# Windowed attention on one core: scores and transposes in smaller tiles, group norm folded into the evacuations, the subtraction of the maxima divided between two engines

## What is computed

```
x = x + L0(gn(x))      # windows of 7x7: layer norm, a linear scan over 49 steps, an MLP with gelu
x = x + L1(gn(x))      # shifted-window attention

# L1, for every 7x7 window (49 tokens) of the image rolled by 3:
qkv  = xw @ qkv_w.T + qkv_b            # 12 heads of 16 channels
attn = (q * 16**-0.5) @ k.T + bias + mask
out  = softmax(attn) @ v
out  = out @ proj_w.T + proj_b         # rolled back
```

## The kernel before, in words

| p | order on TensorE before |
|---|---|
| 0 | scores, transposes, mix 0, turn 0, value group, turn 1 |
| 1 | scores, transposes, project 0, project 1, value group |
| 2 | scores, transposes, project 2, values 0, value group |
| 3 | scores, transposes, values 1, value group, wait for keys and queries, mix 1 |

## Time and profile before

### The profile page before, as it was taken

One profiled execution on the slowest core, in us unless ns is written; L12 is line 12 of the kernel. 1 busy time (PEld: TensorE's weight loads), 2 busy tenths in 40 slices (PEclk: granted clock), 3 DMA queues, 4 the chain that ended last, 5 costly groups with the idle time before them and its releaser, 6 DMA issues. The chain is left out here.

```text
span 4769.8 us, 122473 instructions
## 1 busy us (share of the span) xinstructions
PE 4471.3 (94%) x42440; PEld 3822.0 (80%) x42440; DVE 4085.7 (86%) x7841; ACT 2351.8 (49%) x4594; POOL 2642.9 (55%) x1714
## 2 busy tenths in 40 slices
PE   0599999999999999999969999999999999999998
PEld 0488888888888888888857888888888888888887
DVE  6798888888888888888838888888888888888887
ACT  0244444444444444444415555555555555555555
POOL 1245555455545554555536666666666666666665
PEclk9999999999999999999969999999999999999999
DMA  8011111111111111111112222222222222222222
GB/s 341 21 38 38 39 39 41 37 39 39 41 37 39 39 41 38 38 39 39 37 46 79 80 78 79 81 81 77 80 79 81 77 81 78 82 80 78 79 81 65
DMA packets 398996, 310.66 MB, mean 65 GB/s; under 512 B 140011, under 2 KB 397243, under 8 KB 397755
## 3 DMA queue, kind: packets, MB, share of 16 engines
q1 hardware_dynamic: 396212, 307.89, 21.9%
q10 hardware_dynamic: 2736, 2.14, 0.1%
HBM read 145.48 MB, written 87.33 MB: 49 GB/s over the span
## 5 line engine op out<-in xcount | busy, mean ns | idle before, releaser
L885 POOL TENSOR_TENSOR E<-E,ri 128x588 f32<-128x588 f32 x512 | 802.8, 1568 | 781.5 <-DVE ri L1092 781.5
L604 PE MATMUL ps_o<-w,g_hi 128*128 128x384 f32 x2352 | 709.7, 365 | 5.9 <-DVE g_lo L544 4.1
L416 ACT ACTIVATE gF<-ps_g,b1f 128x512 f32<-128x512 f32 x588 | 404.6, 688 | 392.8 <-PE ps_g L635 390.7
L604 PE MATMUL ps_o<-w,g_lo 128*128 128x192 f32 x2352 | 534.5, 254 | 0.0
L969 ACT ACTIVATE PT<-ps_t 98x588 f32<-98x588 f32 x512 | 338.9, 662 | 395.6 <-PE ps_t L1216 395.6
L1082 DVE SCALAR_TENSOR_TENSOR L<-ps_s,bias 128x588 f32<-128x588 f32 x512 | 394.6, 771 | 152.3 <-PE ps_s L1208 144.2
L1216 PE MATMUL ps_t<-ident,E 128*98 128x128 f32 x3072 | 441.8, 280 | 78.5 <-POOL E L885 78.4
L443 POOL TENSOR_TENSOR res<-xt,b2b 128x768 f32<-128x768 f32 x98 | 181.0, 1847 | 591.1 <-DVE x L492 591.1
L1216 PEld LDWEIGHTS ps_t<-ident,E 128*98 128x98 f32 x3072 | 313.8, 128 | 233.4 <-POOL E L885 198.1
L402 ACT ACTIVATE h_hi<-ps_h,hbias 128x512 fp32r<-128x512 f32 x196 | 123.1, 679 | 703.6 <-PE ps_h L619 703.6
L1208 PE MATMUL ps_s<-Kp,Q 64*64 64x196 f32 x6144 | 455.1, 342 | 2.7 <-DMA Kp<-K 2.7
(11 more groups left out here) (203 smaller groups left out, 12238.8 us busy)
## 6 DMA issues: line engine op xcount, KB each, us to landing
xs<-in_x SPq DMA_DIRECT2D x8, 4704.0 KB, 22.3
xt<-in_x SPq DMA_DIRECT2D x98, 384.0 KB, 3.4
x_cells<-x SPq DMA_DIRECT2D x784, 48.0 KB
xb<-x_cells SPq DMA_DIRECT2D x128, 294.0 KB
Vx<-V SPq DMA_DIRECT2D x512, 73.5 KB
out<-yo SPq DMA_DIRECT2D x128, 294.0 KB
Kp<-K SPq DMA_DIRECT2D x512, 49.0 KB, 1.8
gnr<-gn_rows SPq DMA_DIRECT2D x128, 192.0 KB
```

What stands on the lines that cost most here:

```text
L416: act.activation(gF[f % 4][:, :], ps_g[:, f % 2, :], ACT.Gelu, bias=b1f[:, f:f + 1]).then_inc(s_gelu, 1)
L604: last = pe.matmul(dst, g[:, f, P * k:P * (k + 1)], w, start=(f == 0 and i == 0), stop=(f == FT - 1 and i == 1))
L885: pool.tensor_tensor(e, e, ri[p][:, :].unsqueeze(2).to_broadcast([P, HEADS, T]), ALU.mult)\
```

## The change

- **Scores.** A block is now 2 heads (32 rows, 98 columns): six pairs of heads, two windows, 24 instructions a slot for 12. The pairs' order on the columns is `PAIR_AT`. They come in two parts, places 0, 3, 1, 4 and places 2, 5; the second has a wait for the first (`s_scx`) and gives the semaphore that the bias add waits for (`s_sc`). Between them stand, by slot, mix 0, project 0, project 2 or values 1, and the waits for `s_nm` and `s_ptc`.
- **Transposes.** 12 of 64 rows by 98 columns against a 64-column identity, in place of 6 of 128 rows; each window has its own bank.
- **Group norm.** No normalised copy of x is made. `turn` transposes the loaded x1; the scale goes into `upper` and `lower`, and the shift, projected through the weights once in the setup, comes as the bias of the evacuations (`params`, loaded per unit as 7 numbers a partition). GpSimd's two passes and the table in DRAM are gone; it adds up the bias of oT (`vb`).
- **Maxima.** VectorE takes them off the first 6 heads, GpSimd off the last 6 (`less_max`, right behind the product); the exponential waits for both.
- **ScalarE** takes the last query channels (p = 1) and the first half of the values (now in p = 3).
- The wait of the value group for the bias add of its slot is gone; the wait for keys and queries moves from the end of p = 3 to the start of p = 0.

| p | order on TensorE after |
|---|---|
| 0 | first scores, mix 0, waits, second scores, transposes, turn 0, value group, turn 1 |
| 1 | first scores, project 0, waits, second scores, transposes, project 1, value group |
| 2 | first scores, project 2, waits, second scores, transposes, values 0, value group |
| 3 | first scores, values 1, waits, second scores, transposes, value group, mix 1 |

```diff
+PAIR_AT = (0, 4, 2, 1, 5, 3)
...
-            HB = HEADS // 3
-            QB = 256
+            HB = 2
+            SB = HEADS // 2 * T
...
-            def s_block(b):
-
-                return ps_s[:, :, :].rearrange("p a (b n) -> p (a b) n", n=QB)[:, b, 0:HB * T]
...
+            def s_pair(j):
+
+                return ps_s[:, 2 * j // JP, T2 * (j % (JP // 2)):T2 * (j % (JP // 2) + 1)]
...
-                    act.activation(x_hi[rows, h, :], ps_w(TURN + h)[rows, 0:UW], ACT.Copy).then_inc(s_xh, 1)
+                    act.activation(x_hi[rows, h, :], ps_w(TURN + h)[rows, 0:UW], ACT.Copy,
+                                   scale=par[d][rows, h:h + 1]).then_inc(s_xh, 1)
...
+                def less_max(u, p):
+                    pool.wait_ge(s_mx, UP * u + p + 1)
+                    l = L[p][:, HS:HEADS, :]
+                    pool.tensor_tensor(l, l, mx[p][:, HS:HEADS].unsqueeze(2).to_broadcast([P, HEADS - HS, T]),
+                                       ALU.subtract).then_inc(s_sbp, 1)
...
                             norm(pu, pp)
+                        if is_unit(u):
+                            less_max(u, p)
...
-                        if is_unit(u + 2) and p >= 2:
-
-                            if p == 2:
-                                pool.wait_ge(s_xb[c], 16 * LOADS * (i + 2))
-                                upto(pool, s_tx, 2 * (u + 2))
-                                pool.tensor_tensor(xn[0:T2, :, :], xb[c][0:T2, :, :],
-                                                   gnr[c][0:T2, 0:C].unsqueeze(1).to_broadcast([T2, UP, C]), ALU.mult)\
-                                    .then_inc(s_ns, 1)
-                            else:
-                                pool.wait_ge(s_ns, u + 3)
-                                pool.tensor_tensor(xn[0:T2, :, :], xn[0:T2, :, :],
-                                                   gnr[c][0:T2, C:2 * C].unsqueeze(1).to_broadcast([T2, UP, C]), ALU.subtract)\
-                                    .then_inc(s_nx, 1)
+                        if is_unit(u + 1) and p == 3:
+                            v, d = u + 1, 1 - c
+                            pool.wait_ge(s_qkm, 3 * v + 3)
+                            pool.wait_ge(s_qb, v + 1)
+                            upto(pool, s_o, UP * (v - 1))
+                            pool.tensor_tensor(vb[d][:, :], par[d][:, 5:7], bqkv[:, 3:5], ALU.add).then_inc(s_vb, 1)
...
                             act.wait_ge(s_sub, k + 1)
+                            act.wait_ge(s_sbp, k + 1)
...
+                        if nxt and p == 1:
+                            queries_b(i, c)
...
                             copied(act, i, c)
+                            act.activation(V[0:T2, 0:2, :], v_sum(0), ACT.Copy).then_inc(s_vc[0], 1)
...
                             dve.wait_ge(s_mx, k + 1)
-                            dve.tensor_tensor(L[p][:, :, :], L[p][:, :, :],
-                                              mx[p][:, :].unsqueeze(2).to_broadcast([P, HEADS, T]),
+                            l = L[p][:, 0:HS, :]
+                            dve.tensor_tensor(l, l, mx[p][:, 0:HS].unsqueeze(2).to_broadcast([P, HS, T]),
                                               ALU.subtract).then_inc(s_sub, 1)
...
-                        if nxt and p == 1:
-                            queries_b(i, c)
-                        if nxt and p == 2:
-
-                            dve.wait_ge(s_v, 2 * (u + 1) + 1)
-                            copied(dve, i, c)
-                            dve.tensor_copy(V[0:T2, 0:2, :], v_sum(0)).then_inc(s_vc[0], 1)
...
+                def scores(c, p, places):
+
+                    for j in places:
+                        rows, chunk = pair_rows(PAIR_AT[j])
+                        for w in range(2):
+                            last = pe.matmul(s_pair(j)[SLOT * w:SLOT * (w + 1)], Q[c][rows, chunk, 2 * p + w, :],
+                                             Kp[c][rows, chunk, :, 2 * p + w, :], start=True, stop=True)
+                    return last
+
...
+                        between = is_unit(u - 1) if p == 0 else nxt
                         if is_unit(u):
-
-                            k = UP * u + p
-                            if isinstance(u, int):
-                                upto(pe, s_lg, k)
-                            for w, b in ((0, 0), (0, 2), (1, 0), (1, 2), (0, 1), (1, 1)):
-                                row, chunk = key_block(b)
-                                rows = slice(row, row + HB * HD)
-                                last = pe.matmul(s_block(b)[SLOT * w:SLOT * (w + 1)], Q[c][rows, chunk, 2 * p + w, :],
-                                                 Kp[c][rows, chunk, :, 2 * p + w, :], start=True, stop=True)
-                            last.then_inc(s_sc, 1)
-                        if is_unit(lu):
-                            k = UP * u + p - 2
-                            pe.wait_ge(s_nm, k + 1)
-                            upto(pe, s_ptc, k)
-                            for j in range(JP):
-                                last = pe.transpose(ps_t[0:T2, j // JB, P * (j % JB):P * (j % JB + 1)],
-                                                    E[lp][:, 2 * j:2 * j + 2, :].rearrange("p h m -> p (h m)"),
-                                                    ident[:, :])
-                            last.then_inc(s_pt, 1)
+                            if p == 0:
+                                pe.wait_ge(s_qkm, 3 * u + 3)
+                                pe.wait_ge(s_qb, u + 1)
+                                pe.wait_ge(s_kp[c], 16 * K_SPREADS * (i + 1))
+                            upto(pe, s_lg, UP * u + p)
+                            scores(c, p, (0, 3, 1, 4)).then_inc(s_scx, 1)
                         if is_unit(u - 1) and p == 0:
                             mix(i, c, 0)
                         if nxt:
...
+                        if is_unit(lu):
+
+                            pe.wait_ge(s_nm, UP * u + p - 1)
+                            upto(pe, s_ptc, UP * u + p - 2)
+                        if is_unit(u) and between:
+                            pe.wait_ge(s_scx, UP * u + p + 1)
+                            scores(c, p, (2, 5)).then_inc(s_sc, 1)
+                        if is_unit(lu):
+                            for j in range(JP):
+                                for w in range(2):
+                                    rows = slice(SLOT * w, SLOT * (w + 1))
+                                    last = pe.transpose(ps_t[0:T2, w, SLOT * j:SLOT * (j + 1)],
+                                                        E[lp][rows, 2 * j:2 * j + 2, :].rearrange("p h m -> p (h m)"),
+                                                        ident[rows, rows])
+                            last.then_inc(s_pt, 1)
                         if nxt and p == 0:
                             turn(i, c, 0)
+                        if is_unit(u) and not between:
+                            pe.wait_ge(s_scx, UP * u + p + 1)
+                            scores(c, p, (2, 5)).then_inc(s_sc, 1)
                         if nxt and p == 1:
                             project(i, c, 1)
                         if nxt and p == 2:
...
-                            if is_unit(u):
-
-                                pe.wait_ge(s_lg, UP * u + p + 1)
...
-                        if nxt and p == 3:
-
-                            pe.wait_ge(s_qkm, 3 * (u + 1) + 3)
-                            pe.wait_ge(s_qb, u + 2)
-                            pe.wait_ge(s_kp[1 - c], 16 * K_SPREADS * (i + c + 1))
```

More of the change, by code:

```diff
@@ L940, in evacuated @@
                         upto(act, s_sc, UP * (v - 1))
-                        last = act.activation(Q[d][:, 0, :, 0:T], full, ACT.Identity, bias=bqkv[:, 0:1])
+                        last = act.activation(Q[d][:, 0, :, 0:T], full, ACT.Identity, bias=par[d][:, 2:3])
                     else:
@@ new lines, in _ @@
+                link(dve.memset(params[:, :, :], 0.0))
+                dve.wait_ge(s_e2, 1)
+                for h, rows in enumerate((P, CB)):
+                    dve.tensor_copy(params[0:rows, :, h], ps_e[0:rows, 2 * IMGS * h:2 * IMGS * h + IMGS])
+                    last = dve.tensor_copy(shift2[0:rows, h, :], ps_e[0:rows, 2 * IMGS * h + IMGS:2 * IMGS * (h + 1)])
+                last.then_inc(s_sh2, 1)
+                dve.wait_ge(s_q2, 1)
+                for k in range(5):
+                    rows, dst = CB if k == 4 else P, params[:, :, 2 + k]
+                    projected = ps_q[0:rows, IMGS * k:IMGS * (k + 1)]
+                    if k < 3:
+                        last = dve.tensor_scalar(dst[0:rows], projected, bqkv[0:rows, k:k + 1], None, ALU.add)
+                    else:
+                        last = dve.tensor_copy(dst[0:rows], projected)
@@ L1333 @@
     arrays["b1"] = by_column(inputs["L0_conv_b1"], rows=P)[:, :, 0]
-    def by_dimension(block):
-        return CB * block + np.array([HD * e + d for d in range(HD) for e in range(CB // HD)])
```

(3 more changed lines are left out.)

145 lines of the change are left out of this document (81 added, 64 removed).

## The result

The changed kernel takes **5712.23 us** (median of 4 runs, 5706.61 to 5732.01); the kernel before took 4777.05 beside it. The ratio is 1.197, its 95% interval 1.194 to 1.200: slower, as forecast, but by 935 us where 488 were forecast, and above the top of the range, 5470. The profiled execution took 5732.01 us with a span of 5730.1, 20 us above the median; TensorE's mean granted clock fell from 0.990 to 0.864.

A forecast was written before the change was run, and what follows sets the result against it. TensorE bounds the kernel, a second chain right behind; the change closes a one-slot loop. Slots 5.9 + 4.6 + 4.9 + 6.0 = 21.4 us a unit against 17.63, +483, setup +5: 5265 us, range 5130 to 5470.

The forecast's parts named there:

- what would show it: Signs listed for the attention stage: VectorE busy about 60%, TensorE 77%, full clock, bias adds 5.9, 4.6, 4.9, 6.0 us apart.
- p = 1 to 2: Slot of a unit: TensorE's own path of 4.0 us is shorter than the one-slot loop, so 4.6 us.
- part 6: Savings by engine: transposes 0.5 us (0.31 overlapped, 1.0 if nothing does); TensorE saves little, VectorE's savings mostly idle.
- b: Time from the start of the second score part to the bias add: 0.4 us, bounds 0.3 and 0.6.
- p = 2 to 3: Slot where the exponential waits for GpSimd's half of the maxima (0.89 us, bounds 0.78 and 1.0): 4.9 us.
- p = 3 to 0: Slot of transposes, copy to PT, value group, mix 1, four places and mix 0: 6.0 us.
- part 5: Last slot of a unit: values 1 and mix 0 no longer cover the copy to PT; 6.0 us.
- p = 0 to 1: Slot where project 0 precedes the second scores and needs both lower parts: 5.9 us, against 4.71 before.
- part 7: Setup: bias gather comes after the projected shifts, some 18 small products more; +5 us, bounds 0 and 10.
- (a): Rival: TensorE stays the bound, faster, the wait always met already; 15.9 us a unit, 4560 us; 5%.
- (b): Rival: only the short loop counts, project 0 and PT in time; 18.4 us a unit, 4880 us; 8%.
- (d): Rival: small tiles don't overlap in scores and transposes; 23.4 us a unit, 5520 us at most; 17%.

The follow-up runs named there:

- after_filled: The changed kernel with useless matmuls added where TensorE waits, nothing left out: 5290.96 us, ratio 1.108.
- before_maxima_gpsimd: The kernel before with the whole subtraction of the maxima given to GpSimd: 4838.72 us, ratio 1.014.
- tiles_undone: The changed kernel given back the old score blocks, whole transposes and TensorE's old order: 4779.0 us, ratio 1.0013.
- before_maxima_divided: The kernel before with only the division of the maxima between VectorE and GpSimd: 4751.88 us, ratio 0.995.
- scores_first: The changed kernel with both score parts at the start of the slot, ahead of mix 0, project and values: four executions, 5597.1 to 5856.3 us.
- order_alone: The kernel before with only TensorE's order changed, old blocks and transposes kept, a one-column product carrying the waits: 5577.8 us, ratio 1.168.
- old_order2: The changed kernel with all 24 scores, waits and transposes ahead of mix 0, project and values: 4829.56 us, ratio 1.012.

## Why the prediction was wrong in its size

**The step that failed is the last clause of "what would show it": "TensorE 77% of the stage, all at full clock".** No row bore it out. The earlier trace rows show full clock for a TensorE that is 97% busy, and the forecast took that level over to a TensorE that it had itself given over 4 us of idle time a unit. The sum of its terms holds when the clock does: forecast 5265, after_filled 5291. The missing term is the clock, +421 us (after against after_filled), and more than that beside the filler's own cost: with slots of 6.15, 4.44, 4.62 and 6.00 us a unit at full clock has 21.2 us, an estimated 5240 for the run (4777 + 10 + 3.6 x 127), so the clock costs an estimated 470. At half clock a slot is bound by TensorE, 6.9 us for the 4.6 and 4.9 forecast. The mean unit is 25.0 us for 21.4. VectorE, forecast about 60% busy, is so in after_filled (61%) and not in the changed kernel (52%).

**Term by term, at full clock.**
- *p = 1 to 2*, 4.6 forecast, 4.44 measured. Errors cancel in part: the product 1.26 for 1.57 (part 6 took VectorE's saving as idle, while it freed GpSimd), b 0.47 for 0.4, and the wake some 0.13 for 0.05.
- *p = 2 to 3*, 4.9 forecast, 4.62 in after_filled; 4.44, the length of the loop, in the 78 units of the changed kernel that have full clock there. The half subtraction on GpSimd takes 0.68 for 0.89, below its lower bound of 0.78. The forecast halved a product of 1.57, which is one lengthened by VectorE; from the 1.17 of before_maxima_gpsimd its own formula gives 0.70.
- *p = 3 to 0*, 6.0 forecast, 6.02, and 6.00 in the changed kernel where the clock is full (4082.56 to 4088.56). Nothing covers the copy to PT, as part 5 had it: 1.02 us of waiting.
- *p = 0 to 1*, 5.9 forecast, 6.15 at full clock (4088.56 to 4094.70 in the changed kernel): each lower part takes 0.62 for the 0.56 held unchanged, and the wake of TensorE 0.14 for 0.06. At half clock project 0 alone adds 0.9: from 4013.39 to the scores at 4015.31 1.92 us, for 1.06 forecast; the slot becomes 7.2 (4008.78 to 4015.98).
- *Setup*, +5 forecast, +10: not only the gather, the first unit's transposes too stand 10 us later, 2501.91 for 2491.86 before. That is the upper bound of part 7. The shifts are the 18 products of the forecast (36 instructions in the trace, two a product) and take 6.0 us; they begin at 2464.87, where the gather stood at 2460.8, 1.8 us after the weights' first use on ScalarE in the earlier trace rows. The wait of 4 us and the 6.0 are the 10.
- *Nothing*, for the fold and the evacuations: nearly so, some 20 us beside the setup (tiles_undone against before_maxima_divided).

**The rivals.** (a), TensorE bound and faster, fell: the loop shows in every slot at full clock, and TensorE is the bound only at half clock, to the loss side. (b), the short loop alone, is one part of it: 297 us with old tiles (5070 - 4773), of the 714 that the whole order costs at full clock. The rest comes with project 0, values 1 and mix 0 ahead of the wait. (d) came out beside the point. The 12 transposes take 0.48 us (4008.64 to 4009.12), so they overlap; places 2 and 5 take 0.33. The rows of the transposes' weight loads (first and last start) show the same:

```profile
L1266 PEld LDWEIGHTS ps_t<-ident,E x12: 122/124/128, 4002.7 to 4002.9; 64*98 64x98 f32 x12
```

Each of the twelve loads takes 0.12 us and they start within 0.2 us, so they lie beside one another. The 1.0 us that part 6 gave the transposes "if nothing does" overlap, and with it the 0.5 a unit in (d), is shown by no run; 0.48 us were measured, near the 0.5 of the forecast's sum. The four places and the two of a slot take 0.49 + 0.33 us, the same 0.82 as the 12 large products of the earlier trace rows; small tiles bring the scores as a whole nothing.

**What stays open.** What exactly lets the clock fall was not measured; the runs show that the idle stretches of these orders come with it, that filling them keeps it up, and that it stays down behind a TensorE that is 92 to 96% busy. The profiled scores_first has shorter waits than the changed kernel and fewer of them, yet a lower clock in the stage (0.73 for 0.77), and another execution of it has a higher one (0.876 over the run); that too is unexplained. Why order_alone holds 0.93 with the same order as the changed kernel's 0.77 was not separated from its larger tiles.

## What to carry to other kernels

When a change gives the busiest engine idle time, ask of TensorE whether it keeps its clock, and price the case at a lower clock (0.50 here) as a case of its own; a row that shows full clock at 97% busy did not carry over to a stage with these waits. A test is cheap: fill the waits with useless matmuls, and if the time *falls* with the granted clock back at 1.00 (421 us here), it was the clock. And look at what stands ahead of the instruction that releases a consumer. A wait for another engine there closes a loop through three engines, 4.96 us a slot by itself here; work there lengthens a slot where it ends later than that wait (project 0 in p = 0 to 1, mix 1 and mix 0 in p = 3 to 0), and costs nothing where it ends sooner (project 2 in p = 1 to 2: 4.44 us in after_filled, the length of the loop). The old order releases the consumer first and has TensorE's other work behind the transposes, where it covers the chain.

## What the runs showed that was not expected

- **Adding work made kernels faster**: the changed kernel 5712 to 5291 us (7.4%), scores_first 5597 to 5856 down to 5112 (9 to 13%), order_alone 5578 to 5487 (1.6%), with the clock at 1.00 instead of 0.77, 0.73 and 0.93 in the stage.
- **The length of GpSimd's product depends on VectorE's operation beside it.** Its lengths 1.17, 1.26 and 1.57 us stand against an overlap with the subtraction of 0, 0.24 and 0.55 us. The theory before the last of these runs, 1.02 us and the overlap, asked for 1.02 without any: it fell. The three values fit an estimate: 1.17 us, and where the two overlap the overlap less 0.15 (1.17 - 0.15 + 0.24 = 1.26, 1.17 - 0.15 + 0.55 = 1.57). It was fitted afterwards to these three lengths and not tested; by what the subtraction lengthens the product no run shows.
- **TensorE can wait for itself**: its weight loads for 0.28 us, between two score parts of which the second has a wait for the first and nothing lies between, 445 times in old_order2.
